# Linear attention: output products of a tile on 128x64 tiles and one state update, on one Trainium2 core

## The chip, the core and the metric

The kernel runs on one core of a Trainium2 chip. The metric is device time in microseconds: the median of three timed runs was 1131.69 us (1129.71 to 1132.22). The profile is of one further execution. Engines are named as the profile names them: PE multiplies matrices (PEld is its loading of weights), DVE and ACT are the vector and the scalar engine, POOL works elementwise beside them, SP issues the DMAs.

## The reference

Two layers of adaLN blocks on 2 sequences of 2048 rows of 128 numbers, all in fp32: linear attention with a decaying state and a gate, two layers of windowed attention with gated MLP, then a second attention and a mixture of experts. The change lies in the first of these, the linear attention with 2 heads of 64:

```python
def step(S, inp):
    q_t, k_t, v_t, g_t = inp
    S = S * jnp.exp(g_t)[..., None] + k_t[..., None] * v_t[..., None, :]
    o_t = jnp.einsum('bhk,bhkv->bhv', q_t, S)
    return (S, o_t)
_, o = jax.lax.scan(step, S0, (qh, kh, vh, gh))
...
o = o * jax.nn.sigmoid(gate)
og = og * jax.lax.rsqrt(jnp.mean(og * og, axis=-1, keepdims=True) + EPS)
```

S is 64x64 for each head of each sequence.

## The kernel before

The 4096 rows are 32 tiles of 128 rows; a tile's scan is replaced by products. Each engine has its own program, a fixed list of stages with lags: at step s a stage of lag k works on tile s - k, and the stages of a step run in the written order. Engines meet by semaphores only. On PE a step is: transpose the normalized rows (`turn_h`, L712), `output` of the tile four steps back (L776 to L780), `scores` of lag 3 (L756, products of 64 rows), `values` (L742, L745), the projections (L735), mean squares (L786) and the output projection (L797).

`output` adds three things up for a tile. The carried state, a 128x128 array `la_state` with the two heads' 64x64 blocks on the diagonal and zeros beside them, is multiplied with the decayed queries `la_qe` into 128 columns of PSUM bank 6 (`out`, L776). Then each head's values are multiplied with its attention weights and added into the same columns, one product for partitions 0 to 63 and one for 64 to 127 (L778). Last, the keys decayed to the tile's end (`kendT`) are multiplied with the values into the next 128 columns (L780); of these only the two 64x64 blocks on the diagonal are read. An fp32 product appears as two MATMUL records in the trace.

On DVE, `update` (L462) waits for output, multiplies each head's block of the state with the decay of the tile's last row and adds that head's block of L780: two instructions of 64x64. Behind it stands `gated` (L469), which reads the first 128 columns, and `query` (L435). DVE's order in a step is: statistics of finished rows, base_level (L454), clip (L420, L422), scaled (L442, which makes `la_qe`), residual (L480, two instructions), running_sum (L429), update, gated, query, keep_levels (L449).

ACT's order around the change is: values (L612, copies the values and the turned keys out of PSUM), decays (L627), the next tile's normalized rows (L577), exps, logs and so on. POOL makes keys (L306) and distances (L319 to L328) one step after the running sum, which the decays read three steps behind; in the first twelve steps it also works on the modulation rows (L343 to L355).

Identity products (L183) keep PE running where it would wait; `before_output` issues one of them into bank 6 at step 4, and `output` four before the last tile. They write the identity matrix into each 128 columns of the bank.

From step 32 on, steps of the windowed attention are mixed with the last steps of the linear attention.

Of the kernel before, what the change touches and what calls it, by code (L numbers as in the profile page):

```python
# [20 lines left out]
ALU = mybir.AluOpType  # L21
# [3 lines left out]
P = 128  # L25
B, T, E = 2, 2048, 128
# [8 lines left out]
GH, GD = 2, 64  # L35
# [79 lines left out]
class Core:  # L115
# [15 lines left out]
    def sb(self, ctx):  # L131
        return lambda name, shape, dt=F32: ctx.enter_context(self.nc.sbuf_tensor(name, shape, dt))
# [48 lines left out]
def idle_products(c, bank, n):  # L181
    for _ in range(n):
        c.nc.tensor.matmul(bank[:, 0:BANK].rearrange("p (a b) -> p a b", b=P), c.ident[:, :],  # L183
                           rows_bc(c.ident[:, :], BANK // P), start=True, stop=True)
# [7 lines left out]
def linear_attention(c, y, given, ctx):  # L192
# [4 lines left out]
    nc, inp, bk = c.nc, c.inp, c.bank  # L197
    proj, turn, soft, q_bank, out, wide = bk[0], bk[1], bk[2], bk[3], bk[6], bk[7]
# [12 lines left out]
    with ExitStack() as own:  # L211
# [8 lines left out]
        qe, attn = ring("qe", 3, Q_SLOTS, P), ring("attn", 3, GH, P)  # L220
        sg, vk = ring("sg", 4, 2, P), ring("vk", 4, 2, P)
        state = [sb(f"la_state{b}", [P, P]) for b in range(B)]
        masks = sb("la_masks", [P, NLEV, P], U32)
        keep = sb("la_keep", [P, P])
        dist, dec = ring("dist", 2, 1 + SLOTS * P), ring("dec", 2, SLOTS, P)
# [17 lines left out]
    def in_turn(name, n, every=1):  # L243
        s = sem(name)
        return [Signal(s, k, n, every) for k in range(n)]
# [15 lines left out]
    p_o = signal("p_o")  # L261
    v_st, v_og = in_turn("v_st_og", 2)
# [8 lines left out]
    batch = lambda t: t // NT  # L271
# [5 lines left out]
    value = lambda t: vk[:, t % 4, 0, :]  # L277
    kendT = lambda t: vk[:, (t + 2) % 4, 1, :]
    hd = lambda h: slice(GD * h, GD * h + GD)
# [103 lines left out]
    def vector(dve):  # L383
# [73 lines left out]
        def update(t):  # L457
            p_o.wait(dve, t)
            s_b = state[batch(t)]
            for h in range(GH):  # L460
                s = hd(h)
                last = nc.vector.scalar_tensor_tensor(  # L462
                    out=s_b[s, s], in0=s_b[s, s], scalar=dec[s, t % 2, 0, P - 1:P],
                    in1=out[s, E + GD * h:E + GD * h + GD], op0=ALU.mult, op1=ALU.add)
            last.then_inc(v_st.sem, 1)

        def gated(t):
            p_wo.wait(dve, t - 6)
# [63 lines left out]
        def early(s):  # L532
            def f():
                if 3 <= s <= 5:
                    shift(s - 2)
                if s == 6:
                    output_weights()
                if s in TABLE_STEPS:
                    given.vector(dve, TABLE_STEPS.index(s))
                if s == 10:  # L540
                    more_columns()
            return f

        TABLE_STEPS = (5, 7, 8, 9)
        between = {s: early(s) for s in range(3, 11)}
        return Phase([(y_statistics, 10), (base_level, 4), (clip, 1), (y_shift, 11), (scaled, 3), (residual, 9),
                      (running_sum, 1), (next_statistics, 1), (update, 4), (gated, 4), (query, 1), (keep_levels, 3)], 0, TILES,
                     between=between, begin=begin)

# [137 lines left out]
    def tensor(pe):  # L687
# [8 lines left out]
        def mod_rows(r):  # L696
            k = r // B
            for j, (lo, hi) in enumerate(((0, BANK), (BANK, 6 * E))):
                m = nc.tensor.matmul(bk[ROW_BANKS[r][j]][:, 0:hi - lo], lhs[:, r, :], wmod[:, k, lo:hi],
                                     start=True, stop=True)  # L700
            if r == 2:
                for at in range(2, 12):
                    m = column(*divmod(at, 6), bk[5][:, 2 * P + (at - 2) * B:2 * P + (at - 1) * B])
            m.then_inc(p_set, 1)
# [65 lines left out]
        def output(t):  # L770
            v_og.wait(pe, t - 1)
            if t == TILES - 1:
                idle_products(c, out, 4)
            v_base.wait(pe, t)
            a_vk.wait(pe, t + 2)
            nc.tensor.matmul(out[:, 0:P], state[batch(t)][:, :], qe[:, t % 3, 0, :], start=True, stop=True)  # L776
            for h in range(GH):
                nc.tensor.matmul(out[hd(h), 0:P], value(t)[:, hd(h)], attn[:, t % 3, h, :], start=False,  # L778
                                 stop=True, skip_group_check=True)
            nc.tensor.matmul(out[:, E:2 * E], kendT(t), value(t), start=True, stop=True).then_inc(p_o.sem, 1)  # L780

        def mean_squares(t):
            a_sq.wait(pe, t)
# [30 lines left out]
        def early(s):  # L814
            def f():
                if s == 2:
                    pe.wait_ge(a_set, ROW_COPIES[0])
                mod_rows(s + 1)
            return f
# [2 lines left out]
            pe.wait_ge(a_set, REST)  # L822
            idle_products(c, bk[4], 1)

        def before_output():
            pe.wait_ge(a_set, ROW_COPIES[1])
            idle_products(c, out, 1)

        def before_products():
            pe.wait_ge(v_set, WOG[0])  # L830

        return Phase([(while_waiting, 4), (turn_h, 0), (after_turn, 0), (output, 4), (scores, 3), (values, 1), (after_values, 0),
                      (project, 0), (mean_squares, 5),
                      (o_project, 8)], 0, TILES, longer=values, more=2,
                     between={1: early(1), 2: early(2), 3: before_scores, 4: before_output, 8: before_products}, begin=begin)

    last = TILES - 1
    left = {0: (v_q, last), 1: (a_rr, last), 2: (a_s, last), 3: (v_prod, last), 4: (v_base, last), 5: (v_base, last),
            6: (v_res[1], last), 7: (v_res[1], last)}
    return (sync, gpsimd, vector, scalar, tensor), left  # L840


# [1705 lines left out]
```

## Time and profile before

| what | value |
|---|---|
| timed runs, median (range) | 1131.69 us (1129.71 to 1132.22) |
| the profiled execution, its own time | 1124.29 us |
| its span, first to last instruction | 1122.5 us |
| PE busy over the span | 1042.4 us (93%) |
| DVE / ACT / POOL busy | 879.7 / 843.3 / 672.7 us |
| state products L776, records, mean | 64, 287 ns |
| attention products L778 | 128, 298 ns |
| key-value products L780 | 64, 326 ns |
| state updates L462 | 64, 271 ns |

A busy time is the sum of the stretches in which an engine had an instruction in work, and the means are from start to end of one record. Records of PE overlap, so the distance from one record's start to the next is shorter than a record.

### The profile page before, as it was taken

To read this page: it belongs to the slowest core of one execution; us is meant where nothing else is said; L and a number is where in the kernel's file an instruction comes from. 1 tells how busy PE (TensorE), PEld (TensorE's weight loads), DVE (VectorE), ACT (ScalarE), POOL (GpSimd) and SP (SyncE) were. 2 spreads that over 40 slices of the span, in tenths; PEclk is the share of its full clock that TensorE was granted. 3 is DMA by queue.
4 is the path that set the end of the run, shared out by engine and by line. 5 is a ranking of instruction groups with operands and counts; after the bars stand their busy time and mean duration, and the time that the engine had idled before them with its cause. 6 is when DMAs were issued, how large, how long until landed. Compare 5 with 4: busy or idle time off the path is not lost. (4 is left out here: it accounts for less than half of the span.)

```text
span 1122.5 us, 33918 instructions
## 1 busy us (share of the span) xinstructions
PE 1042.4 (93%) x11723; PEld 717.4 (64%) x11723; DVE 879.7 (78%) x2963; ACT 843.3 (75%) x2678; POOL 672.7 (60%) x1080
## 2 busy tenths in 40 slices
PE   6989998889999999899899999998998899999995
PEld 3667775467777776566577777776566588844442
DVE  4999996678888888664888888887685635299998
ACT  5788884599999998433799999997356867388986
POOL 4999995789889888210888988987243300012223
PEclk9999999999999999999999999999999999999999
DMA  7000000112222212321112221221001343000000
GB/s 245 7 2 12 12 2 2 29 39 56 60 57 57 47 45 47 105 73 35 42 39 50 49 49 40 50 49 42 20 1 41 98 137 84 11 10 15 17 18 19
DMA packets 66498, 50.86 MB, mean 45 GB/s; under 512 B 42262, under 2 KB 53442, under 8 KB 66050
## 3 DMA queue, kind: packets, MB, share of 16 engines
q1 hardware_dynamic: 66339, 48.84, 17.1%
q8 instruction: 88, 1.44, 0.6%
q14 instruction: 71, 0.58, 0.2%
HBM read 21.41 MB, written 2.38 MB: 21 GB/s over the span
## 5 line engine op out<-in xcount | busy, mean ns | idle before, releaser
L1258 PE MATMUL psum<-wa_wqkv,wa_hT 128*128 128x512 f32 x384 | 188.1, 597 | 1.3 <-DVE wa_tmp L1123 1.3
L1215 ACT ACTIVATE wa_p<-psum,wa_nb 128x128 f32<-128x128 f32 x512 | 184.7, 404 | 0.0
L1104 POOL TENSOR_TENSOR wa_p<-wa_p,wa_rrs 128x512 f32<-128x512 f32 x128 | 133.5, 1043 | 10.1 <-DVE wa_rrs L1148 10.1
L1811 POOL TENSOR_TENSOR ex_total<-ex_total,mod 128x128 f32<-128x128 f32 x32 | 15.6, 486 | 204.1 <-DVE ex_total L1939 204.1
L1139 DVE CUSTOM_DVE_ANT_0 psum<-psum,wa_bias 128x128 f32<-128x128 f32 x512 | 132.1, 320 | 5.3 <-PE psum L1296 5.2
L1215 ACT ACTIVATION_READ_ACCUMULATOR wa_p<-psum,wa_nb 128x1 f32 x512 | 125.2, 244 | 0.0
L1986 ACT ACTIVATE cv_z_ex_yw<-psum,ex_w 128x128 f32<-128x128 f32 x384 | 107.1, 401 | 19.8 <-DVE ex_w L1915 7.3
L2057 PE MATMUL psum<-ex_wc,ex_hT 128*128 128x512 f32 x256 | 117.7, 603 | 3.5 <-DVE cv_z_ex_yw L1922 2.1
L1080 POOL TENSOR_TENSOR wa_kr<-wa_kr,wa_tmp 128x512 f32<-128x512 f32 x64 | 81.8, 1277 | 41.6 <-DVE wa_tmp L1123 41.6
L1225 ACT ACTIVATE wa_pT<-psum 128x512 f32<-128x512 f32 x128 | 78.4, 612 | 31.9 <-PE psum L1272 31.8
L1091 POOL TENSOR_TENSOR wa_qr<-wa_qr,wa_rn 128x512 f32<-128x512 f32 x64 | 66.8, 1044 | 56.7 <-ACT wa_rn L1197 56.7
L2057 PEld LDWEIGHTS psum<-ex_wc,ex_hT 128*128 128x128 f32 x256 | 45.2, 189 | 65.8 <-issue 65.1
L1123 DVE TENSOR_TENSOR wa_tmp<-psum,wa_tabs 128x512 f32<-128x512 f32 x128 | 87.0, 680 | 0.0
L1075 POOL TENSOR_TENSOR wa_qr<-wa_qr,wa_tmp 128x512 f32<-128x512 f32 x64 | 81.6, 1275 | 5.1 <-DVE wa_tmp L1123 5.1
L1258 PEld LDWEIGHTS psum<-wa_wqkv,wa_hT 128*128 128x128 f32 x384 | 63.3, 192 | 33.2 <-issue 32.7
L1154 DVE COPY wa_oT<-psum 128x512 f32<-128x512 f32 x64 | 44.2, 690 | 50.8 <-PE psum L1311 50.6
L1272 PE MATMUL psum<-ident,wa_p 128*128 128x128 f32 x512 | 80.6, 280 | 0.1
L1586 ACT ACTIVATE ml_gelu<-psum,ml_b 128x512 f32<-128x512 f32 (+1 forms) x48 | 32.9, 685 | 63.2 <-PE psum L1617 53.9
L1939 DVE TENSOR_TENSOR cv_z_ex_yw<-cv_z_ex_yw 128x1024 f32<-128x1024 f32 (+2 forms) x96 | 78.3, 816 | 1.8 <-ACT cv_z_ex_yw L1986 0.8
L1294 PE MATMUL psum<-wa_kT,wa_qT 64*64 64x128 f32 x1024 | 71.0, 277 | 9.1 <-ACT wa_p L1215 8.9
L1130 DVE TENSOR_REDUCE wa_ss<-wa_sq 128x16 f32<-128x1024 f32 x64 | 76.0, 1188 | 0.0
L1311 PEld LDWEIGHTS psum<-wa_pT,wa_vm 128*64 128x64 f32 x1024 | 52.1, 137 | 34.9 <-issue 34.9
(264 smaller groups left out, 3039.4 us busy)
## 6 DMA issues: line engine op xcount, KB each, us to landing
wa_vm<-wa_v SPq DMA_DIRECT2D x127, 128.0 KB, 2.4
cv_toep<-cv_zpad SPq DMA_DIRECT2D x32, 136.0 KB, 2.7
cv_toep<-cv_zpad SPq DMA_DIRECT2D x16, 264.0 KB, 4.1
wa_tabs<-in_rotations_dram SPq DMA_DIRECT2D x2, 2048.0 KB, 7.9
wa_rows<-y_rows SPq DMA_DIRECT2D x31, 128.0 KB
wa_rows<-y_rows SPq DMA_DIRECT2D x31, 127.0 KB
x_rows<-in_L_attn_x_dram SPq DMA_DIRECT2D x4, 512.0 KB, 5.8
out_dram<-x_rows SPq DMA_DIRECT2D x32, 64.0 KB, 1.5
```

What stands on the lines that cost most here:

```text
L1075: nc.gpsimd.tensor_tensor(q, q, tmp[:, t % 2, 0, :], ALU.add).then_inc(g_q.sem, 1)
L1080: nc.gpsimd.tensor_tensor(k, k, tmp[:, t % 2, 1, :], ALU.add).then_inc(g_k.sem, 1)
L1104: nc.gpsimd.tensor_tensor(p, p, cols_bc(rrs[:, t % 2, r, :], P), ALU.mult)\
L1123: nc.vector.tensor_tensor(halves(heads(cross)), halves(src)[:, :, ::-1, :], halves(rows_bc(sin, WH)), ALU.mult).then_inc(done.sem, 1)
L1139: m = nc.vector.tensor_tensor_reduce(out=s, in0=s, in1=edges, scale=-1.0, scalar=MAX_FLOAT, op0=ALU.add, op1=ALU.min, accum_out=nb[:, t % ...
L1215: e = nc.scalar.activation(pr[:, t % 2, r, h, :], sim_bank[r][:, P * h:P * h + P], ACT.Exp, bias=nb[:, t % 2, r, h:h + 1], scale=-1.0, acc ...
L1225: nc.scalar.activation(flat(pT[:, t % 2, r, :, :]), p_bank, ACT.Copy)\
L1258: nc.tensor.matmul(bank, hT[:, t % 3, :], wqkv[:, INNER * k:INNER * k + INNER], start=True, stop=True).then_inc(done.sem, 1)
L1272: m = nc.tensor.transpose(bank[:, P * k:P * k + P], src(t, k), c.ident[:, :])
L1939: nc.vector.tensor_tensor(to, y[:, 0:n, :], y[:, n:2 * n, :], ALU.add).then_inc(v_half[k].sem, 1)
L1986: m = nc.scalar.activation(yw[:, t % 2, e, :], up_banks[(4 * t + k) % 6][:, P * j:P * j + P], ACT.Relu, scale=w[:, t // GT % 2, t % GT, e: ...
L2057: nc.tensor.matmul(up_banks[number % 6], hT[:, t // GT % 3, t % GT, :], wc[:, batch(t), chunk(k)], start=True, stop=True).then_inc(p_up[k] ...
```

## The change

Output issues the key-value product first, and only its two diagonal blocks: one 64x64 product for each head, each into the 64 partitions of its head. The state product is split by columns of the state into two, each for 64 partitions of the result. So all six products of a tile have the form of the two attention products, 128 rows by 64 columns of weights. The state update is one instruction on 128x128. It needs zeros in the blocks beside the diagonal of the second 128 columns; they are those that the identity products leave there, and the function that issues the first of these has a new name.

```diff
         def update(t):
             p_o.wait(dve, t)
             s_b = state[batch(t)]
-            for h in range(GH):
-                s = hd(h)
-                last = nc.vector.scalar_tensor_tensor(
-                    out=s_b[s, s], in0=s_b[s, s], scalar=dec[s, t % 2, 0, P - 1:P],
-                    in1=out[s, E + GD * h:E + GD * h + GD], op0=ALU.mult, op1=ALU.add)
-            last.then_inc(v_st.sem, 1)
+            nc.vector.scalar_tensor_tensor(out=s_b[:, :], in0=s_b[:, :], scalar=dec[:, t % 2, 0, P - 1:P],
+                                           in1=out[:, E:2 * E], op0=ALU.mult, op1=ALU.add).then_inc(v_st.sem, 1)
...
             v_base.wait(pe, t)
             a_vk.wait(pe, t + 2)
-            nc.tensor.matmul(out[:, 0:P], state[batch(t)][:, :], qe[:, t % 3, 0, :], start=True, stop=True)
             for h in range(GH):
-                nc.tensor.matmul(out[hd(h), 0:P], value(t)[:, hd(h)], attn[:, t % 3, h, :], start=False,
-                                 stop=True, skip_group_check=True)
-            nc.tensor.matmul(out[:, E:2 * E], kendT(t), value(t), start=True, stop=True).then_inc(p_o.sem, 1)
+                nc.tensor.matmul(out[hd(h), E + GD * h:E + GD * h + GD], kendT(t)[:, hd(h)], value(t)[:, hd(h)],
+                                 start=True, stop=True)
+            for h in range(GH):
+                nc.tensor.matmul(out[hd(h), 0:P], state[batch(t)][:, hd(h)], qe[:, t % 3, 0, :], start=True,
+                                 stop=True)
+            for h in range(GH):
+                m = nc.tensor.matmul(out[hd(h), 0:P], value(t)[:, hd(h)], attn[:, t % 3, h, :], start=False,
+                                     stop=True, skip_group_check=True)
+            m.then_inc(p_o.sem, 1)
...
-        def before_output():
+        def zeros_between_heads():
             pe.wait_ge(a_set, ROW_COPIES[1])
             idle_products(c, out, 1)
```

What stands on PE in step 8, before. The names are result <- operands and the size of the result; 64x128 x2 are the two heads, and L756 are the scores behind output:

```order
L712 MATMUL psum<-ident,la_rows 128x128 [waits la_a_n,la_v_set]
L776 MATMUL psum<-la_qe,la_state 128x128 [waits la_a_vk,la_v_base,la_v_st_og]
L778 MATMUL psum<-la_attn,la_vk 64x128 x2
L780 MATMUL psum<-la_vk 128x128
L756 MATMUL psum<-la_qe,la_dec 128x128 [waits la_v_prod,la_v_base]
L756 MATMUL psum<-la_qe,la_dec 128x128 x3
```

And at the same place in the changed kernel:

```order
L708 MATMUL psum<-ident,la_rows 128x128 [waits la_a_n,la_v_set]
L773 MATMUL psum<-la_vk 64x64 [waits la_a_vk,la_v_base,la_v_st_og]
L773 MATMUL psum<-la_vk 64x64
L776 MATMUL psum<-la_qe,la_state 64x128 x2
L779 MATMUL psum<-la_attn,la_vk 64x128 x2
L752 MATMUL psum<-la_qe,la_dec 128x128 [waits la_v_prod,la_v_base]
L752 MATMUL psum<-la_qe,la_dec 128x128 x3
```

The key-value product has moved from the end of the group to its front, with the group's waits, and both it and the state product are two instructions now.

DVE around the update in step 10, before (L442 is scaled, L449 keep_levels):

```order
L442 TENSOR_TENSOR la_qe<-la_dec,psum 128x768 [waits la_p_o,la_v_scan_q,la_a_dec]
L480 SCALAR_TENSOR_TENSOR x_rows<-psum,la_rr,x_rows 128x128 [waits la_a_log_rr,la_p_wo]
L480 SCALAR_TENSOR_TENSOR x_rows<-psum,la_rr,x_rows 128x128 [waits la_v_res]
L429 SCALAR_TENSOR_TENSOR la_dist<-la_ones,psum 128x128 [waits la_a_kend,la_a_dec,la_a_l]
L462 SCALAR_TENSOR_TENSOR la_state<-la_state,la_dec,psum 64x64 [waits la_p_o]
L462 SCALAR_TENSOR_TENSOR la_state<-la_state,la_dec,psum 64x64
L469 TENSOR_TENSOR la_ogT<-psum,la_sg 128x128
L435 TENSOR_TENSOR psum<-psum,la_sg 128x128 [waits la_v_prod,la_a_s]
L449 TENSOR_TENSOR la_attn<-psum,la_keep 128x256 [waits la_p_o,la_p_att]
```

And in the changed kernel:

```order
L442 TENSOR_TENSOR la_qe<-la_dec,psum 128x768 [waits la_p_o,la_v_scan_q,la_a_dec]
L476 SCALAR_TENSOR_TENSOR x_rows<-psum,la_rr,x_rows 128x128 [waits la_a_log_rr,la_p_wo]
L476 SCALAR_TENSOR_TENSOR x_rows<-psum,la_rr,x_rows 128x128 [waits la_v_res]
L429 SCALAR_TENSOR_TENSOR la_dist<-la_ones,psum 128x128 [waits la_a_kend,la_a_dec,la_a_l]
L460 SCALAR_TENSOR_TENSOR la_state<-la_state,la_dec,psum 128x128 [waits la_p_o]
L465 TENSOR_TENSOR la_ogT<-psum,la_sg 128x128
L435 TENSOR_TENSOR psum<-psum,la_sg 128x128 [waits la_v_prod,la_a_s]
L449 TENSOR_TENSOR la_attn<-psum,la_keep 128x256 [waits la_p_o,la_p_att]
```

One instruction stands where two stood; nothing else on DVE has moved, and ACT's and POOL's orders are as before.

## Rows read from the trace of the kernel before

**Rows 1.** Busy time by stretch: us, PE, PEld, DVE, ACT, POOL, granted clock, DMA

```profile
41.50:76.30 34.80, 31.84 (x406) 23.50 (x405) 33.37 (x92) 27.20 (x65) 33.73 (x97) 1.00 0.01 2
80.00:160.00 80.00, 74.28 (x979) 56.34 (x977) 76.31 (x239) 68.91 (x184) 72.27 (x249) 1.00 0.04 9
```

**Rows 2.** Waits, 80 to 160 us: us in total, times, longest

```profile
ACT la_vk L612 <- PE psum L745: 10.7, 17, 0.7
POOL la_key L306 <- DVE la_dist L429: 6.3, 16, 1.2
PE psum L712 <- ACT la_rr L643: 2.9, 4, 0.7
PE psum L712 <- ACT la_rows L577: 2.8, 12, 0.2
...
DVE la_dist L429 <- ACT psum L598: 1.3, 4, 0.3
```

**Rows 3.** Timeline of one step, PE: start, us, engine, line

```profile
107.39 0.33 PE L712 MATMUL psum<-ident,la_rows 128*128 128x128 f32 x1 [0.23 <-ACT la_rows L577]
107.55 0.39 PE L776 MATMUL psum<-la_qe,la_state 128*128 128x128 f32 x2
107.88 0.44 PE L778 MATMUL psum<-la_attn,la_vk 128*64 128x128 f32 x4
108.25 0.49 PE L780 MATMUL psum<-la_vk 128*128 128x128 f32 x2
108.67 1.23 PE L756 MATMUL psum<-la_qe,la_dec 64*128 64x128 f32 x36
...
109.99 0.39 PE L745 MATMUL psum<-la_wv,la_hT 128*128 128x128 f32 x2
110.21 0.39 PE L735 MATMUL psum<-la_hT,la_wk 128*128 128x128 f32 x2
...
112.07 0.33 PE L712 MATMUL psum<-ident,la_rows 128*128 128x128 f32 x1 [0.24 <-ACT la_rows L577]
```

**Rows 4.** Timeline, PE in the windowed attention: products on 128x64 tiles

```profile
303.72 0.34 PE L1311 MATMUL psum<-wa_pT,wa_vm 128*64 128x64 f32 x4
303.89 0.29 PE L1311 MATMUL psum<-wa_pT,wa_v 128*64 128x64 f32 x4
304.00 0.29 PE L1311 MATMUL psum<-wa_pT,wa_vm 128*64 128x64 f32 x4
```

**Rows 5.** Timeline of the same step, DVE

```profile
107.90 0.73 DVE L480 SCALAR_TENSOR_TENSOR x_rows<-psum,la_rr,x_rows 128x128 f32<-128x128 f32 x2
108.55 0.42 DVE L429 TENSOR_TENSOR_SCAN la_dist<-la_ones,psum 128x128 f32<-128x128 f32 x1
108.88 0.55 DVE L462 SCALAR_TENSOR_TENSOR la_state<-la_state,la_dec,psum 64x64 f32<-64x64 f32 x2
109.46 0.29 DVE L469 TENSOR_TENSOR la_ogT<-psum,la_sg 128x128 f32<-128x128 f32 x1
```

**Rows 6.** Timeline at 76 us, POOL and ACT

```profile
76.09 0.29 POOL L328 TENSOR_TENSOR la_dist<-la_dist 128x64 f32<-128x64 f32 x1
...
76.89 0.95 ACT L627 ACTIVATE la_dec<-la_dist 128x896 f32<-128x896 f32 x1
```

**Rows 7.** State products (L776) from 78 to 166 us: durations, first and last start

```profile
L776 PE MATMUL psum<-la_qe,la_state x38: 275/278/337, 78.9 to 165.4; 128*128 128x128 f32 x38
```

**Rows 8.** Timeline of the last outputs, PE and DVE

```profile
175.96 1.23 PE L756 MATMUL psum<-la_qe,la_dec 64*128 64x128 f32 x36 [0.32 <-DVE la_qe L442]
...
188.60 0.49 PE L776 MATMUL psum<-la_qe,la_state 128*128 128x128 f32 x2 [0.77 <-DVE la_attn L454]
...
189.92 0.57 DVE L462 SCALAR_TENSOR_TENSOR la_state<-la_state,la_dec,psum 64x64 f32<-64x64 f32 x2 [0.74 <-PE psum L780]
```

**Rows 9.** Busy time by stretch behind the linear attention, columns as in rows 1

```profile
188.60:192.00 3.40, 2.32 (x14) 1.56 (x15) 2.37 (x9) 0.31 (x1) 2.01 (x5) 1.00 0.01 2
192.00:195.40 3.40, 3.39 (x6) 1.90 (x7) 0.00 (x0) 0.48 (x1) 0.00 (x0) 0.51 0.00 0
```

## What is predicted

> **What bounds the kernel now.** I read the busy times by stretch first [rows 1]. The change touches only the linear attention, whose last output products run at 188.60 us [rows 8]; the rest of the 1122.5 us span has none of the edited instructions, and what the linear stage ends earlier it starts earlier. In that stage PE, DVE and POOL are each busy for 90 to 95% of 80 to 160 us, so a busy share names no bound. The list of waits of the same stretch does [rows 2]: DVE waits for next to nothing (1.3 us of 80); PE waits for ACT at the transpose that opens a step (L712); ACT waits for PE at the copy of the values (L612: 10.7 us in 17 waits, 0.63 each); POOL waits for the running sum of DVE (6.3 us in 16 waits, 0.39 each).
>
> One step in order of time [rows 3] shows how these close into a loop. PE transposes at 107.39 and runs output (L776, L778, L780), scores (L756) and values (L745); ACT waits for the last of these, copies (L612), then does the decays and the normalized rows, and PE's next transpose waits for those rows at 112.07. The turn is 4.68 us with a wait at each change of engine and no slack inside, and the output products are in it: 107.55 to 108.67, that is 1.12 us, or 1.28 from the transpose to the scores. DVE has a second loop of the same length, its own program order, because it hardly waits; the state update (L462) is in that one. So there are two loops of 4.68 us, and the change shortens a piece of each. Over 18 steps the mean is (165.4 - 78.9) / 18 = 4.8 us [rows 7], since every fourth step PE waits up to 0.7 us for two small ACT instructions (la_rr, rows 2).
>
> **PE, part by part.** A product of 128 columns inside one tile shape takes 0.22 us (L745 to L735, 109.99 to 110.21). Output before: the state product takes 0.33, the two 128x64 products together 0.37, the key-value product 0.42 [rows 3]. Each is followed by another shape (128x64, 128x128, then the 64-row scores), and the 0.11 above 0.22 is what a change of shape costs; the rest is weights that are loaded in the open behind it. Where 128x64 products follow one another (L1311, 64 columns each, a pair as x4), the first pair behind a change of shape takes 0.17 and the next 0.11 to 0.12 [rows 4]; so both column tiles work at the same time, and their weights load behind the products before.
>
> Output after: the transpose and its change of shape 0.16 + 0.11 = 0.27; two key-value products of 64 columns, as the first L1311 pair, 0.17; the two state products, 128 columns side by side, 0.22; the two attention products 0.22, and the change to the scores 0.11. Sum 0.99 against 1.28: the PE loop loses 0.29 us. Bounds: if the 128x64 tiles of one pair ran in turn, the three pairs would cost 0.05 + 0.22 + 0.22 more and nothing would be gained; if the changes of shape cost nothing at all, 0.77 would stand and 0.51 be gained. I take 0.29, because L778 in this very place has the form of the new products and runs four records in 0.37.
>
> A rule speaks against this. The Trainium skill ("TensorE: Matmul & The Clock Gate", "The mechanism") says that a weight load overlaps running products only if it goes to other rows of the array, and all six new products use all 128 rows. In rows 4 a pair behind its own kind takes 0.12 and the first 0.17, so the 0.05 of an open load is not paid again: the trace disagrees. By the rule six loads of 0.05 would be open, 0.99 would become 1.29, and PE would gain nothing (rival 3).
>
> The waits of output now stand on the key-value product, the first of the group; they are the same three, and the signal to DVE still follows the last product, so nobody is held longer. The renamed function issues the instruction it issued before, and no DMA, POOL or ACT instruction is added or moved.
>
> **DVE.** Before, from the first update to the gated product is 108.88 to 109.46, 0.58 us for two instructions of 64x64 [rows 5]. After, one instruction of 128x128. The nearest row is the residual (L480, the same operation on 128x128 with one operand in PSUM): two of them take 0.73 with a wait between, 0.37 each; L429 starts 0.65 behind the first, so 0.65 - 0.37 = 0.28 behind the second. The update takes between 0.28 (the next instruction not held) and 0.37 (held as by a wait). I take 0.28 and save 0.30, because most neighbours in rows 5 overlap by 0.08 (L429 starts at 108.55, 0.08 before the end of the second L480; L462 starts at 108.88, 0.09 before the end of L429) and only the gated product behind L462 starts 0.03 after its end. Zero is the bound below, if the wider instruction took all of 0.58.
>
> The Trainium skill ("VectorE: DVE Perf Modes", "Two Vector instructions with no wait between them") says that an instruction is held until the earlier ones are done when an operand starts in another quarter of the partitions than the one before it. The second 64x64 update starts at partition 64 and the gated product at 0 again, and there the trace has the gap: it agrees. With one update from partition 0 nothing is held, and by this rule the sum stays as it is; by another section of the same page, "The DRAIN you can't avoid", which has every instruction wait for the pipe to empty, the step would save 0.21.
>
> **Together.** The PE and ACT loop loses 0.29, the DVE loop 0.30, so a step loses 0.29. What is late next: POOL waits 0.39 of each step of 4.8 [rows 2], so it needs 4.4; the new mean is 4.5, and POOL keeps 0.1. ACT keeps more.
>
> Where it counts: from 41.5 to 76.3 POOL is busy 33.73 of 34.80 us [rows 1] (it also makes the modulation rows there); the steps cannot get ahead of it. Its distances for the decays at 76.89 end at 76.38 (L328, 76.09 + 0.29) [rows 6], so up to that point the gain is held to 0.5, whatever the nine outputs before 78.9 save. Then come 18 whole turns (38 records, two to a product, are 19 products) [rows 7]: 18 x 0.29 = 5.2; and one more turn that starts with the last of them, 0.3. Of the four outputs behind it I count three at nothing: attention work is mixed in, and PE waits for the scaled queries (175.96) with the output done [rows 8]. The last one (188.60) has DVE waiting for its end at 189.92, with the update on the way to the next output projection: 0.29 + 0.30 = 0.6. Sum 0.5 + 5.2 + 0.3 + 0.6 = 6.6 us. The profiled execution took 1124.29 us (span 1122.5 and 1.8 around it), 7.4 below the median of the timed runs; I take the 6.6 off both: 1117.7 in a profile like this one, 1131.69 - 6.6 = 1125.1 us in the timed runs.
>
> **Rivals.**
> 1. DVE becomes the bound. The update costs 0.37, its loop loses 0.21, and DVE has no wait to give back [rows 2]. 18 x 0.21 + 0.5 + 0.2 + 0.5 = 5.0: 1126.7 us; if the wider update took all of 0.58, only the 0.5 and the 0.3 of the last product would stand, 1130.9. For it: the one gap in rows 5 stands right behind the update. Against: the gap has a reason that the edit takes away.
> 2. The tiles of a pair run in turn. The loop through ACT stays at 4.68, DVE's shorter update turns into a wait for the scores, and 0.3 at the end remains: 1131.4 us, no change that can be measured. Against: the four records of L778 in 0.37.
> 3. The weight loads of the six products are open, 0.05 each: again PE gains nothing, 1131.4 us. Against: rows 4, where every pair behind the first takes 0.12. The rule of the Trainium skill on loads, above, would do this.
> 4. Slower: PE's clock falls. PE ran at half clock from 192.0 to 195.4 after it had been busy 2.32 of 3.40 us [rows 9]. The place where it could happen anew is 41.5 to 76.3: POOL sets the pace, so what output saves becomes PE idle time, 7 steps of 0.29, and PE's 31.8 busy of 34.8 us [rows 1] would be 29.8. A stretch of 3.4 us at half clock does 1.7 us less work. With the 6.6 gained elsewhere four such stretches cancel the gain and six end 3.6 slower: 1135.3 us. Against: rows 1 show the full clock in both stretches, and 2 us spread over seven steps leave no long gap. The Trainium skill ("TensorE: Matmul & The Clock Gate", "What's actually happening") says that the throttle is the default and activity lifts it; the low stretch behind the idle one agrees.
> 5. More: POOL's modulation rows don't hold the early steps, and all 32 outputs pay 0.30: 9.6 us, 1122.1 us.
>
> **Numbers.** Forecast 0.70 (its own range 1121.5 to 1128: a step loses 0.2 to 0.5, and about 1 us of spread between runs), rival 1 0.12, rival 2 0.06, rival 3 0.04, rival 4 0.05, rival 5 0.03. A measurement of this kernel tells 0.2% (2.3 us) from no change. The forecast, rival 5 and nearly all of rival 1 are faster: 0.84; rivals 2 and 3 and the far end of rival 1 make 0.11; rival 4 0.05. The range 1121.0 to 1129.5 leaves out rivals 2 to 4, 0.15.
>
> **What would show it.** Right: the two 64-column products in about 0.17, transpose to scores about 1.0 instead of 1.28, one update with the gated product 0.28 behind it, ordinary steps of about 4.4 us, the wait of ACT for the values still there, output products between 78 and 165 us moved ahead by up to 5 us and little gained before 76 us. Wrong: the pairs start one behind the other; the gap behind the update stays; POOL without any wait through the whole stage; a granted clock of half inside 30 to 188 us.

## The result, and the profile after

The changed kernel takes 1120.53 us in the median of four runs (1120.0 to 1120.85), the kernel before, run beside it, 1130.70 (1129.23 to 1132.22). The ratio is 0.9927, with a 95% interval of 0.9906 to 0.9947: faster, by more than the 0.2% that a measurement of this kernel can tell. On the 1131.69 us from which the forecast was made the ratio gives 1123.4 us (1121.1 to 1125.7); the forecast was 1125.1, with a range from 1121.0. The median itself lies 0.5 us under that range.

The same step of the linear attention in the timeline of the changed kernel, TensorE alone (start, us, engine, line), to be read against [rows 3]:

```profile
104.89 0.33 PE L708 MATMUL psum<-ident,la_rows 128*128 128x128 f32 x1 [0.24 <-ACT la_rows L573]
105.15 0.34 PE L773 MATMUL psum<-la_vk 128*64 128x64 f32 x4
105.31 0.39 PE L776 MATMUL psum<-la_qe,la_state 128*64 128x128 f32 x4
105.54 0.39 PE L779 MATMUL psum<-la_attn,la_vk 128*64 128x128 f32 x4
105.85 1.23 PE L752 MATMUL psum<-la_qe,la_dec 64*128 64x128 f32 x36
...
109.26 0.33 PE L708 MATMUL psum<-ident,la_rows 128*128 128x128 f32 x1 [0.24 <-ACT la_rows L573]
```

From the transpose to the scores it is now 0.96 us instead of 1.28: 0.26 to the key-value pair, 0.16 for that pair, 0.23 and 0.31 for the two others, the change to the scores in the last. The turn is 4.37 us instead of 4.68. The transpose still waits 0.24 for ACT's rows, so the loop through ACT is still closed.

The same stretch on VectorE, against [rows 5]; the two L420 are one turn of its program order apart:

```profile
108.33 0.35 DVE L420 TENSOR_SCALAR la_u<-psum,la_delta 128x128 f32<-128x128 f32 x1
...
110.77 0.32 DVE L460 SCALAR_TENSOR_TENSOR la_state<-la_state,la_dec,psum 128x128 f32<-128x128 f32 x1
111.00 0.28 DVE L465 TENSOR_TENSOR la_ogT<-psum,la_sg 128x128 f32<-128x128 f32 x1
111.30 0.30 DVE L435 TENSOR_TENSOR psum<-psum,la_sg 128x128 f32<-128x128 f32 x1
111.51 0.41 DVE L449 TENSOR_TENSOR la_attn<-psum,la_keep 128x256 f32<-128x256 f32 x1
...
112.69 0.35 DVE L420 TENSOR_SCALAR la_u<-psum,la_delta 128x128 f32<-128x128 f32 x1
```

The gated product (L465) starts 0.23 behind the update, before 0.58. But L435 then follows L465 by 0.30, where it followed by 0.21: the gap that stood behind the update has moved on by one instruction. VectorE's turn is 112.69 - 108.33 = 4.36 us.

The waits from 80 to 160 us (us in total, times, longest), against [rows 2]:

```profile
ACT la_vk L608 <- PE psum L741: 4.4, 14, 0.4
...
PE psum L708 <- ACT la_rr L639: 2.8, 4, 0.7
PE psum L708 <- ACT la_rows L573: 2.6, 12, 0.2
DVE la_dist L429 <- ACT psum L594: 0.8, 3, 0.3
POOL la_key L306 <- DVE la_dist L429: 0.7, 1, 0.7
```

ACT's wait for the values fell from 0.63 a time to 0.31, by as much as the loop; POOL's wait for VectorE is nearly used up. Busy time by stretch, columns as in [rows 1]:

```profile
41.50:76.30 34.80, 29.94 (x435) 22.25 (x434) 33.41 (x85) 27.57 (x66) 33.73 (x98) 1.00 0.01 2
80.00:160.00 80.00, 74.32 (x1114) 56.73 (x1098) 77.17 (x236) 74.80 (x196) 77.22 (x269) 1.00 0.04 9
```

Up to 76 us the busy times of VectorE and POOL are what they were and TensorE's is 1.9 lower: there the products got shorter and the steps hardly did. At 76 us, against [rows 6], the decays start 0.51 earlier, now 0.04 behind the end of POOL's last distance (before 0.51 behind it):

```profile
76.05 0.29 POOL L328 TENSOR_TENSOR la_dist<-la_dist 128x64 f32<-128x64 f32 x1
...
76.38 0.95 ACT L623 ACTIVATE la_dec<-la_dist 128x896 f32<-128x896 f32 x1
```

The last output, against [rows 8]:

```profile
182.09 0.34 PE L773 MATMUL psum<-la_vk 128*64 128x64 f32 x4 [0.77 <-DVE la_attn L454]
...
182.91 0.35 DVE L460 SCALAR_TENSOR_TENSOR la_state<-la_state,la_dec,psum 128x128 f32<-128x128 f32 x1 [0.25 <-PE psum L779]
183.17 0.28 DVE L465 TENSOR_TENSOR la_ogT<-psum,la_sg 128x128 f32<-128x128 f32 x1
```

It starts 6.51 us earlier than before (188.60), its gated product 7.35 earlier (190.52 before). From its first product to the update it takes 0.82 us instead of 1.32. In the windowed attention behind the stage all work runs 7.46 us earlier:

```profile
296.26 0.34 PE L1312 MATMUL psum<-wa_pT,wa_vm 128*64 128x64 f32 x4
```

This is the pair that started at 303.72 in [rows 4]. The lead stays 7.46 from 220 to 520 us. Then TensorE's clock takes some of it back (stretch, us, busy PE, PEld, DVE, ACT, POOL, granted clock, DMA):

```profile
526.30:529.71 3.41, 1.27 (x4) 0.30 (x2) 3.41 (x6) 1.68 (x5) 2.75 (x5) 1.00 0.08 18
529.71:536.54 6.83, 6.03 (x17) 3.14 (x21) 3.23 (x5) 2.48 (x6) 4.68 (x6) 0.50 0.15 35
```

TensorE was busy for 1.27 of 3.41 us and then ran 6.83 us at 1.2 GHz instead of 2.4; the kernel before had no such stretch there. The lead falls to 4.64, and another 0.9 goes between 936 and 960 us in the convolution stage, at full clock. So the profiled executions differ by 3.75 us (1124.29 to 1120.54, spans 1122.5 and 1118.7), though the stage gave 7.46.

The timed runs differ by more than that because the profiled execution of before was among its fastest. A straight line through 29 later runs of before, span against granted clock, gives a span of 1126.4 us at the mean clock of the four runs after (0.989); their spans have a mean of 1118.7. At like clock the kernels are 7.8 apart, about what the stage gave; single runs scatter by 1.2 us about the line. The other 2.4 of the 10.2 us between the two medians are not explained: the clocks of the four runs of before are not on record.

### The profile page after: what moved, and what is told of

Read it like the earlier page. It is cut to its first block and busy times, and to the rows that moved or that the text cites. A ratio compares the mean times of both kernels' runs of the same rounds, so it can differ in the third digit from the quotient of the medians.

```text
span 1118.7 us, 34142 instructions
## 1 busy us (share of the span) xinstructions
PE 1036.0 (93%) x11851; PEld 712.4 (64%) x11851; DVE 873.4 (78%) x2931; ACT 844.8 (76%) x2678; POOL 672.1 (60%) x1080
```

## The experiments

**One edit without the other.** If two loops of nearly one length bound the step, neither edit alone gives much. First the new products with the old update:

```diff
-            nc.vector.scalar_tensor_tensor(out=s_b[:, :], ...
+            for h in range(GH):
+                s = hd(h)
+                last = nc.vector.scalar_tensor_tensor(out=s_b[s, s], ...
```

> The products of the changed kernel, with the state update of before (two instructions of 64x64). Theory A (two loops of equal length, one through PE and ACT, one in DVE's order; both had to be shortened): DVE needs its 0.58 us again, its loop is the bound at about 4.63 us, ordinary steps between 80 and 160 us take 4.60 to 4.65 instead of 4.37, DVE waits for nothing, ACT's wait for the values grows; about 1127.5 us (1126 to 1130). Theory B (the PE loop alone counts, DVE has room): 4.37 as in the changed kernel, 1120.5 us. Theory C (DVE's loop alone counts): 4.68, 1130.7 us.

Measured: 1124.0 us (12 runs, 1120.44 to 1129.71), ratio to before 0.9962 (0.994 to 0.9983); the kernel before took 1129.44 us beside this run and the next three. The timeline of TensorE and VectorE over one step:

```profile
107.48 0.33 PE L712 MATMUL psum<-ident,la_rows 128*128 128x128 f32 x1
...
108.68 1.23 PE L756 MATMUL psum<-la_qe,la_dec 64*128 64x128 f32 x36 [0.17 <-DVE la_qe L442]
...
110.64 0.46 PE L735 MATMUL psum<-la_hT,la_wk 128*128 128x128 f32 x2 [0.26 <-DVE psum L435]
...
112.08 0.33 PE L712 MATMUL psum<-ident,la_rows 128*128 128x128 f32 x1
...
106.99 0.35 DVE L420 TENSOR_SCALAR la_u<-psum,la_delta 128x128 f32<-128x128 f32 x1
...
111.59 0.35 DVE L420 TENSOR_SCALAR la_u<-psum,la_delta 128x128 f32<-128x128 f32 x1
```

The step is 4.60, and the closed loop has changed hands: the transpose waits for nobody, and the scores and the projections (L735) wait for VectorE, whose turn is 111.59 - 106.99 = 4.60 without a wait inside. So VectorE's own loop is 4.60 with two updates. With one it is 4.36: in the changed kernel each distance between its instructions, but for those around the update, is to 0.01 us what it is here, where VectorE waits for nobody. The expectation had ACT's wait for the values grow; it fell to 2.1 us in 10 waits, and ACT has waits for VectorE instead (before its exps, L593: 2.4 us in 9). The median is below the expected range, 1.3 us of it because the kernel before was that much faster than in the runs that the expectation started from. At like clock, by the line above, the two kernels are 3.4 us apart, near the 3.2 expected, but made up in another way: every fourth step fell from 5.19 to 4.83, just as in the changed kernel, so TensorE's edit pays there without the other. From the tenth tile's decays to the thirtieth's the 15 ordinary steps gave 1.64 us and the 5 longer ones 1.76.

Then the old products with the new update (the state outside the two heads' blocks is then not zero):

> The products of before with the one update of 128x128; the blocks of the state beside the diagonal are then not zero, so the linear attention computes another thing than the reference. Theory A: the loop through PE and ACT stays at 4.68, DVE's 0.3 us turn into a wait of keep_levels for the scores in every step; ordinary steps 4.68, 1130 us (1129 to 1131). Theory B: the same, with DVE idle by a further 0.3. Theory C: 4.37, about 1121 us.

Measured: 1127.42 us (12 runs), ratio 0.9976 (0.9962 to 0.9991). One step:

```profile
107.37 0.33 PE L708 MATMUL psum<-ident,la_rows 128*128 128x128 f32 x1 [0.23 <-ACT la_rows L573]
...
112.05 0.33 PE L708 MATMUL psum<-ident,la_rows 128*128 128x128 f32 x1 [0.23 <-ACT la_rows L573]
...
109.92 0.42 DVE L449 TENSOR_TENSOR la_attn<-psum,la_keep 128x256 f32<-128x256 f32 x1 [0.23 <-PE psum L752]
```

The step is 4.68 to the last digit: what the update saves is spent waiting for the scores. The stage gains 0.48 us in all, at its last output. The median is 2 us lower than that of before, and under the 1129 to 1131 expected. Its twelve runs had a higher mean clock than the runs of before (0.990 against 0.988), which by the line above is worth 1.3 us, and no row of the stage shows more than the 0.48. Together the two runs settle it: before, TensorE's loop was 4.68 and VectorE's 4.60; after, they are 4.37 and 4.36.

**The change of tile shape put back.** The state product whole, on 128x128, between the two kinds of pairs:

```diff
-            for h in range(GH):
-                nc.tensor.matmul(out[hd(h), 0:P], state[batch(t)][:, hd(h)], ...
+            nc.tensor.matmul(out[:, 0:P], state[batch(t)][:, :], qe[:, t % 3, 0, :], start=True, stop=True)
```

> The changed kernel with the state product on 128x128 again, between the two kinds of 128x64 products: two changes of shape are back, the columns of the key-value product stay halved. Theory A (a change of shape costs about 0.1 us and opens the next weight load, 0.05 to 0.1): transpose to scores about 1.25 to 1.3, as before the change; steps 4.65 to 4.7, 1129.5 us (1128 to 1131). Rival E (the gain is the halved columns of the key-value product, 0.11 us of streaming, and the shapes cost nothing): transpose to scores 0.95 to 1.0, steps 4.37, 1120.5 us.

Measured: 1127.33 us (12 runs), ratio 0.9987 (0.9972 to 1.0003), no change. One step of TensorE:

```profile
105.54 0.33 PE L708 MATMUL psum<-ident,la_rows 128*128 128x128 f32 x1 [0.23 <-ACT la_rows L573]
105.80 0.34 PE L773 MATMUL psum<-la_vk 128*64 128x64 f32 x4
106.06 0.49 PE L775 MATMUL psum<-la_qe,la_state 128*128 128x128 f32 x2
106.48 0.44 PE L777 MATMUL psum<-la_attn,la_vk 128*64 128x128 f32 x4
106.85 1.23 PE L752 MATMUL psum<-la_qe,la_dec 64*128 64x128 f32 x36
...
110.25 0.33 PE L708 MATMUL psum<-ident,la_rows 128*128 128x128 f32 x1 [0.23 <-ACT la_rows L573]
```

The same columns, with one product of another shape among them: the key-value pair takes 0.26 instead of 0.16, the state product 0.42 instead of 0.23, transpose to scores 1.31. All of TensorE's gain is lost, though half the key-value columns are still saved. The step is 4.71. The median lies 0.7 us under the range expected.

**The order of the pairs.** The key-value pair last, as the product stood before:

> The changed kernel with the key-value products as the last pair of the group instead of the first. Theory A (shapes and columns decide, not the order): transpose to scores 0.95 to 1.0 as before the move, steps 4.37 to 4.40, 1120.5 us (within 1 us). Rival D (the first place counts, since the pair runs while something else is loaded or waited for): transpose to scores longer by the 0.17 of the pair, steps 4.5 and over, 1123.5 us.

Measured: 1121.16 us (6 runs, 1116.82 to 1125.09), ratio 0.9932 (0.9906 to 0.9958). One step of TensorE:

```profile
104.76 0.33 PE L708 MATMUL psum<-ident,la_rows 128*128 128x128 f32 x1 [0.23 <-ACT la_rows L573]
...
105.72 1.23 PE L752 MATMUL psum<-la_qe,la_dec 64*128 64x128 f32 x36
...
109.12 0.33 PE L708 MATMUL psum<-ident,la_rows 128*128 128x128 f32 x1 [0.23 <-ACT la_rows L573]
```

Transpose to scores is 0.96 and the step 4.36, as with the pair in front. The order is worth nothing that can be measured.

**What held the steps before 76 us.** The prediction said POOL. Its ten operations on the modulation gates were cut to 8 of 128 columns, in both kernels:

```diff
-            mags = m[:, :, :, 2, :]
+            mags, part = m[:, :, :, 2, 0:8], sign[:, :, :, 0:8]     # part stands for sign[...] below
```

> The kernel before, with the sign and floor of the modulation gates worked out for 8 of 128 columns alone (its output is then not the reference's): POOL loses ten operations of 1.27 to 1.94 us, one a step, of steps 1 to 11, and nothing else changes. Theory P (POOL, back to back until 76 us in both kernels, is what kept the change from paying in the early steps): steps before 76 us are then set by VectorE, which had 33.37 us busy of 34.80, so decays of tile 9 come about 1.0 us earlier than in the kernel before (0.5 to 1.4). Rival Q (VectorE's own extra work there, four table products of 1.4 us and the columns of 1.0 and 0.5, held the steps): decays of tile 9 come at most 0.3 earlier.

> The changed kernel with the same cut of POOL's work (8 of 128 columns of the gates; its output is not the reference's). Theory P: freed of POOL, the early steps give their 0.3 each as the later ones do, so decays of tile 9 come 2.0 us earlier than in the kernel before with the same cut (1.5 to 2.6), where with POOL's full work the two kernels differ by 0.35 to 0.52 there; the linear attention stage then ends 9.0 us earlier than the other's (8.6 to 9.6) instead of 7.46. Rival Q: the difference at tile 9 stays at most 0.6 and the end of the stage at 7.5.

Each of the two kernels ran once. I compare by the start of the decays, from the third tile to the tenth (seven steps), which leaves out what the clock does at 20 to 30 us. In the kernel before, the cut gains 0.85 us over these steps (35.07 to 34.22), within the range of theory P. But between the two kernels P fails: with POOL's full work the changed kernel gains 0.13 us over these steps (35.07 against 34.94), with the cut 0.53 (34.22 and 33.69), where theory P asked for some 2 and rival Q for at most 0.6. POOL did hold one step, the one into the ninth tile, 5.55 and 5.57 us with its full work, 4.68 and 4.64 without, in both kernels alike. The five steps ahead of it stayed at 4.7 to 5.2. A look at one of them, in the kernel before with light POOL:

```profile
49.07 1.27 DVE L948 SCALAR_TENSOR_TENSOR wa_tabs<-wa_tabs,wa_scales 128x1024 f32<-128x1024 f32 x1
49.22 1.28 POOL L327 TENSOR_TENSOR la_dist<-la_key,la_dist 128x64 f32<-128x64 f32 x1
50.47 0.29 POOL L328 TENSOR_TENSOR la_dist<-la_dist 128x64 f32<-128x64 f32 x1
50.72 0.30 POOL L327 TENSOR_TENSOR la_dist<-la_key,la_dist 128x64 f32<-128x64 f32 x1
```

One distance of POOL that takes 0.30 takes 1.28 while VectorE works out a table for the windowed attention. The distance ends 0.16 behind the table product (50.50 and 50.34). So the table product costs VectorE its own time and holds POOL up too. The Trainium skill ("SBUF — State Buffer", "Who interferes with whom") has a rule for it: an instruction of VectorE with two inputs in SBUF and one of POOL that reads SBUF exclude each other, and the one that comes second is blocked until the first has finished. Here VectorE's came first, and these rows agree in that the distance ends only behind it. Next both were cut, again in one execution of each kernel, the table products to 64 of 1024 columns (one part of sixteen; the expectation says eight):

```diff
-        self.scale_table(dve, k)
+        self.scale_table(dve, k, 1)      # 64 of 1024 columns
```

> The kernel before with POOL's gates cut to 8 of 128 columns and, besides, VectorE's four table products of the linear attention's steps cut to one of eight parts (its output is not the reference's). Theory R (the early steps were held by VectorE's table products and by POOL's gates, each in its own steps and in both kernels alike): from the third step to the tenth every step is 4.6 to 4.7 us, but every fourth up to 5.2. Rival S (something else holds them: statistics of the rows, the start's loads): steps of 4.9 to 5.0 remain where they stood with the gates alone cut.

> The changed kernel with the same two cuts (its output is not the reference's). Theory R: its early steps are 4.35 to 4.45 us (every fourth 4.8 to 4.9), so that from the third tile's decays to the tenth's it gains 2.2 us on the other (1.8 to 2.5), where with the gates alone cut it gained 0.53 over them; the stage ends 9.5 us ahead (9.0 to 10.0) after taking off what the two differ by at the third tile. Rival S: at most 1.0 between these tiles, 8.2 at the end.

The decays of the third and the tenth tile, of before (L627) and of the changed kernel (L623), both with the two cuts:

```profile
38.23 0.94 ACT L627 ACTIVATE la_dec<-la_dist 128x896 f32<-128x896 f32 x1
71.63 0.94 ACT L627 ACTIVATE la_dec<-la_dist 128x896 f32<-128x896 f32 x1
```

```profile
37.07 0.94 ACT L623 ACTIVATE la_dec<-la_dist 128x896 f32<-128x896 f32 x1
68.41 0.94 ACT L623 ACTIVATE la_dec<-la_dist 128x896 f32<-128x896 f32 x1
```

33.40 against 31.34: the change now gains 2.06 over the seven steps, and they are the steps of the later part, 4.68 and 4.36 to 4.43 (5.20 and 4.83 every fourth; one early step took 4.80 in the one, another 4.63 in the other). Theory R holds. To the last tile's decays the gain is 8.51 beyond the third tile's, with the full work 6.29; at the last output's gated product it is 9.34, within the 9.0 to 10.0 of theory R. The two can't be compared beyond that: the kernel before had half-clock stretches there and the other had none. The table products alone were not cut, so how the two share the early steps stays open.

**The clock.** Eight idle products in TensorE's long gaps behind the linear attention, in the changed kernel:

```diff
+                if first == 0 and t in (1, 2):
+                    idle_products(c, p_bank, (3, 2)[t - 1])
...
-            turn_q = turn(..., "turn", turn_bank, a_qT, p_tq)
+            turn_q = turn(..., "turn", turn_bank, a_qT, p_tq, TILES, 3)
```

> The changed kernel with idle products of 0.6 us each put in the long gaps of TensorE behind the linear attention: 3 ahead of the scores of the window attention's tile 1 (gap 205.73 to 208.28), 2 ahead of tile 2's (218.19 to 220.27), 3 ahead of the second layer's first turned queries (527.57 to 529.74). Theory H (the granted clock fell to 0.5 at 208.86 and 529.71 because TensorE had idled there): no stretch at 0.5 within 200 to 225 and 525 to 545, median 1116.5 us (1114.5 to 1118.5), and less spread. Rival I (the clock falls all the same, somewhere near, and the idle products delay real ones): 1120.5 or more.

Measured: 1117.96 us (4 runs, 1116.31 to 1119.66), ratio 0.991 (0.9884 to 0.9937). The two places by stretch:

```profile
207.80:212.20 4.40, 4.40 (x41) 2.25 (x40) 1.58 (x5) 3.84 (x16) 1.91 (x5) 1.00 0.08 18
525.90:529.00 3.10, 3.00 (x8) 1.32 (x9) 3.10 (x5) 0.79 (x2) 2.76 (x3) 1.00 0.08 17
529.00:533.00 4.00, 3.22 (x15) 1.77 (x14) 3.37 (x5) 1.74 (x6) 3.65 (x4) 1.00 0.09 21
```

The clock stays at 1.00 in both. Against the profile after, this one gains 1.64 us at 208 to 215 and 2.63 at 530 to 540, as theory H has it, and loses 2.4 at the start, where its clock was at half from 19.84 to 30.08 us instead of 21.12 to 24.54. The median lies in the range of theory H, but the spread did not shrink: 3.35 us over four runs, where the changed kernel's four lay within 0.85. Nor are two places at full clock in one profile proof that the idle products did it. The changed kernel with the key-value pair last has no half-clock stretch between 523 and 550 us without any idle product, and of the ten profiles without them four have none there and two none between 205 and 235.

Last, the two together, key-value pair last and the idle products:

> The key-value pair last of the six products, as in the run of that order, with the eight idle products in TensorE's gaps. Theory A (the order of the pairs is worth nothing, since VectorE's own 4.36 us are the step as well): 1117 us, within 1.5 of the kernel with idle products alone (1115.5 to 1119). Rival B (the order itself saves time, 0.01 a step and more at the end): 1114.5 or less.

Measured: 1118.3 us (4 runs), ratio 0.9902 (0.9868 to 0.9936): theory A. Its profile, too, has the full clock in both places. The mean granted clock of the eight runs with idle products is 0.990 to 0.996, that of the ten runs of the changed kernel and of the order of the pairs 0.983 to 0.994. That speaks for theory H. But the intervals of both overlap that of the changed kernel (0.9906 to 0.9947), so that either beats it is not shown by the times.

## Why the prediction was right, point by point

- **TensorE's loop.** Said: transpose to scores 0.99 instead of 1.28, a step 0.29 shorter. Measured 0.96 and 0.31. The price of a change of shape was right where it stood (0.26 to the first pair, said 0.27; 0.16 for the pair, said 0.17). That this price is the mechanism is shown by the state product put back whole (1.31).
- **VectorE's loop.** Here a step failed: "two loops of 4.68 us" was wrong. VectorE's was 4.60, and 0.08 of each turn was a wait too small for the list of waits. It saved 0.24, not 0.30, because 0.09 of the gap came back behind the next instruction. The two errors cancel by luck, 4.36 beside 4.37, so the sum did not suffer.
- **Every fourth step** was taken as an ordinary one with a wait. It lost 0.36 instead of 0.29, and from TensorE's edit alone.
- **The sum.** Said 0.5 up to 76 us, 5.5 over the turns that follow, 0.6 for the last output, 6.6 in all. Measured 0.51; 6.2 (from 0.52 to 6.72 over 19 steps, 0.33 each); and 0.94 at the end, less 0.20 that was lost at the last two tiles' decays: 7.46. The terms that were mis-sized are the step (0.29 for 0.33) and the last output (0.6 for 0.94): from its first product to the update it gained 0.50 us, where the step's 0.29 had been put in. POOL, said to keep 0.1 us of each step, has one wait of 0.7 left in 80 us; the prediction named a POOL without any wait as a sign of being wrong, and it came near.
- **Before 76 us** the number was right and its reason was half of it. The lead was 0.04 us at the ninth tile's decays and came in the two steps that follow. The decays of the changed kernel stand right behind POOL's last distance at the eleventh tile alone (0.04); at the six tiles ahead they start 0.39 us or more behind it. Taking its gates away frees one step; VectorE's table products, which also hold POOL up, have to go too.
- **The rivals.** VectorE as the bound (1): it is level with TensorE's loop, and the update was not held for 0.37. Tiles of a pair in turn (2) and open weight loads (3): no, the pairs follow by 0.16 to 0.23. The rule on loads in the Trainium skill ("TensorE: Matmul & The Clock Gate", "The mechanism") would have cost TensorE's whole gain; here the trace disagrees with it. The prediction left out that the same section also lets a load into the background weight buffer run ahead, which these rows don't contradict. A slower clock (4): 1.00 in 41.5 to 76.3 us, as the forecast had it, but a half-clock stretch appeared at 529.71, a place that the rival had not named, and it cost 2.8 us of the profiled execution. Half clock also stood at 184.96 to 188.37 us, inside the 30 to 188 us that were named as a sign of being wrong; it is the stretch that before began at 192.04, come earlier with the work. All 32 outputs pay (5): no.
- **The time.** The 7.4 us between the profiled execution and the median of before was carried over to the time after. It did not hold: the profiled run after took 1120.54, the median of its runs. That, and the 0.9 us more in the stage, put the median under the range; by the ratio the time is inside it (1123.4). Why 0.9 us were lost between 936 and 960 us is open; no run was made for it.

## What to carry to other kernels

Where two engines' loops are within 0.1 us of each other, shortening the longer one alone gives no more than that in the steps that both bound (here 0.08), and shortening the other alone gives nothing there; look for the edit that shortens both, and test them apart. On TensorE, count changes of tile shape before columns: here six products on one shape took 0.32 us less than four on two shapes, and a single odd one among them cost all of it. A gain won in one stage need not reach the end: here a half-clock stretch behind it took 2.8 of 7.46 us in one execution. Compare executions at like granted clock before a few us are put down to an edit.

## What was not expected of the hardware

- While VectorE ran a table product of 1.27 us, a POOL operation of 0.30 took 1.28. With the table product cut to 0.41 us the same operation took 0.31.
- The number and length of the half-clock stretches changed from execution to execution, in kernels alike up to there: between 19 and 31 us there was none, or one of 3.4 or 10.2 us, worth up to 2.7 us (the third tile's decays started at 36.73 with none, at 39.44 with 10.2). The 29 runs of before in one session went from 1124.12 to 1132.71.
- Behind one 128x128 update the next instruction started after 0.23 us, 0.09 before the update's end in the records, and the instruction after that followed 0.09 later than it used to: a gap on VectorE can move instead of going away. Why it moved, no run shows.
